# Cross-attention of a decoder layer: all eight key blocks split into high and low parts, three probability buffers, two copies on VectorE's queue

## The reference

```python
query = _layernorm(x)                       # (4, 512, 512)
Q = (query @ Wq).reshape(b, 512, 4, 4, 32)  # 16 query heads in 4 groups
K = (ctx @ Wk).reshape(b, 1024, 4, 32)      # 4 key heads
V = (ctx @ Wv).reshape(b, 1024, 4, 32)
scores = einsum('bqghd,bkgd->bghqk', Q / sqrt(32), K) + m * rel   # a slope for each head
scores = where(mask, scores, neg)
w = softmax(scores, axis=-1)
out = einsum('bghqk,bkgd->bqghd', w, V).reshape(b, 512, 512) @ Wo
x = x + out
```

## Time and profile before

| | us |
|---|---|
| three runs, median (lowest to highest) | 1869.34 (1868.5 to 1874.75) |
| profiled execution, its own time | 1871.28 |
| its span, first to last instruction | 1869.4 |

### The profile page before, as it was taken

One profiled execution on the slowest core, in us unless ns is written; L12 is line 12 of the kernel. 1 busy time (PEld: TensorE's weight loads), 2 busy tenths in 40 slices (PEclk: granted clock), 3 DMA queues, 4 the chain that ended last, 5 costly groups with the idle time before them and its releaser, 6 DMA issues. The chain is left out here.

```text
span 1869.4 us, 24714 instructions
## 1 busy us (share of the span) xinstructions
PE 1663.9 (89%) x8118; PEld 1161.0 (62%) x8118; DVE 1163.6 (62%) x1997; ACT 1213.6 (65%) x1979; POOL 1177.1 (63%) x1080
## 2 busy tenths in 40 slices
PE   6999999999999958999999999999999606999996
PEld 3588888888888735556555655566656302666664
DVE  2366666666766536666855576556757266677764
ACT  2366666656665524887876687667869344788775
POOL 0478777877877503675755576556757306888892
PEclk9999999999999978999999999999999958999999
DMA  6100000000000055112210311120100080010000
GB/s 215 46 12 12 13 20 16 12 12 24 12 7 12 6 171 138 31 26 76 57 43 26 88 31 40 32 49 18 43 23 23 29 315 0 12 35 27 31 18 24
DMA packets 47103, 85.40 MB, mean 46 GB/s; under 512 B 7548, under 2 KB 12028, under 8 KB 45952
## 3 DMA queue, kind: packets, MB, share of 16 engines
q1 hardware_dynamic: 45136, 82.67, 14.3%
q10 hardware_dynamic: 1840, 1.14, 0.2%
HBM read 52.26 MB, written 12.58 MB: 35 GB/s over the span
## 5 line engine op out<-in xcount | busy, mean ns | idle before, releaser
L1146 POOL TENSOR_TENSOR x_p_lo<-x_p,x_p_hi 128x1024 fp32r<-128x1024 f32 x192 | 455.4, 2384 | 300.2 <-ACT x_p_hi L980 299.5
L1095 DVE TENSOR_REDUCE x_maxes<-x_ps_a 128x1 f32<-128x1024 f32 x256 | 313.1, 1223 | 258.1 <-PE x_ps_a L1229 257.2
L958 ACT ACTIVATE x_p<-x_ps_b,x_any_valid 128x1024 f32<-128x1024 f32 x256 | 284.9, 1113 | 168.5 <-PE x_ps_b L1217 167.8
L1217 PE MATMUL x_ps_b<-x_Q,x_K 100*128 100x512 f32 x512 | 228.1, 526 | 3.7 <-ACT x_p L958 2.2
L980 ACT ACTIVATE x_p_hi<-x_p 128x1024 fp32r<-128x1024 f32 x192 | 203.1, 1058 | 4.8
L1229 PE MATMUL x_ps_a<-x_K,x_Q 99*128 99x512 f32 x512 | 166.3, 406 | 6.8 <-DMA x_Q<-x_p_lo 3.9
L1255 PE MATMUL x_ps_o<-x_p_hi,x_V 128*96 128x512 f32 x384 | 157.1, 409 | 1.2 <-POOL x_p_lo L1146 1.2
L1256 PE MATMUL x_ps_o<-x_p_lo,x_V 128*96 128x512 f32 x384 | 150.9, 393 | 0.0
L1217 PEld LDWEIGHTS x_ps_b<-x_Q,x_K 100*128 100x128 f32 x512 | 90.1, 191 | 97.3 <-issue 76.1
L331 ACT ACTIVATE a_work<-a_ps_s,a_neg_max,a_q_r 128x256 f32<-128x256 f32 (+1 forms) x256 | 134.0, 538 | 4.7 <-DVE a_neg_max L419 4.7
L1260 PE MATMUL x_ps_o<-x_p,x_V 128*96 128x512 f32 x256 | 120.4, 591 | 0.0
(11 more groups left out here) (256 smaller groups left out, 4300.9 us busy)
## 6 DMA issues: line engine op xcount, KB each, us to landing
a_w_raw<-in_L_attn_out_w SPq DMA_DIRECT2D x8, 1024.0 KB, 7.8
x_ctxT<-in_ctx SPq DMA_DIRECT2D x8, 1024.0 KB, 7.3
x_Q<-x_q_hi SPq DMA_DIRECT2D x104, 64.0 KB, 2.0
a_xt<-in_x SPq DMA_DIRECT2D x16, 256.0 KB, 2.8
x_scratch<-a_work SPq DMA_DIRECT2D x16, 256.0 KB, 2.0
x_xt<-x_scratch SPq DMA_DIRECT2D x16, 256.0 KB, 3.6
x_K<-x_k_hi SPq DMA_DIRECT2D x32, 128.0 KB, 2.3
x_x1t<-x_scratch SPq DMA_DIRECT2D x16, 256.0 KB, 3.0
```

Of the source, the lines that this page charges most:

```text
L958: act.activation(p[:, r, :, :], ps_b[:, :, :], ACT.Exp, scale=any_valid[:, b % 2:b % 2 + 1]).then_inc(exp_ready, 1)
L1095: dve.tensor_reduce(out=maxes[:, h2, r, 3:4], in_=ps_a[:, :, :], axis=mybir.AxisListType.XY, op=ALU.max)\
L1146: pool.tensor_tensor(out=p_lo[:, r], in0=p[:, r], in1=p_hi[:, r].bitcast(F32), op=ALU.subtract).then_inc(lo_ready, 1)
L1217: last = pe.matmul(ps_b[:, j, :], K[0:ROWS + 4, g, kb * P:(kb + 1) * P], Q[0:ROWS + 4, hh, :], start=True, stop=True)
```

## The change

Four things, all in `phase_cross_attention`:

1. The last two key blocks are treated as the other six: `V` holds eight blocks, `V32` is gone, and at r = 3 ScalarE rounds, GpSimd subtracts and TensorE makes four fp32r matmuls in place of the fp32 ones.
2. `p` has three buffers in place of four, taken in turn over all units, and `p_hi` and `p_lo` have four in place of three. The exponential of a unit waits for the subtraction three units back.
3. The two 32x512 copies that end a head are made by VectorE with `tensor_copy` (function `copies`) at r = 3, before the reciprocal, in place of ScalarE.
4. The mask row lies in rows of `pv_lo` that nothing else uses. It keeps its waits and its two DMAs for each group.

```diff
-        V = sb("V", [P, 2, 6, GX, 3 * DH], F32R)
-        V32 = sb("V32", [P, 2, 2, GX, 3 * DH])
+        V = sb("V", [P, 2, KB, GX, 3 * DH], F32R)
-        p = sb("p", [P, 4, 2, T])
-        p_hi = sb("p_hi", [P, 3, 2, T], F32R)
-        p_lo = sb("p_lo", [P, 3, 2, T], F32R)
+        p = sb("p", [P, 3, 2, T])
+        p_hi = sb("p_hi", [P, 4, 2, T], F32R)
+        p_lo = sb("p_lo", [P, 4, 2, T], F32R)
...
@@ scalar
-                    if c and r < 3:
-                        act.wait_ge(lo_ready, 3 * (c - 1) + r + 1)
-                    if c and r == 3:
-                        act.wait_ge(pv_done, 4 * c)
-                    act.activation(p[:, r, :, :], ps_b[:, :, :], ACT.Exp, ...
+                    if v >= 3:
+                        act.wait_ge(lo_ready, v - 2)
+                    act.activation(p[:, v % 3, :, :], ps_b[:, :, :], ACT.Exp, ...
...
-                if r == 3 and c >= 1:
...
-                    act.activation(pv_lo[0:DH, :], ps_o[k % 2][DH:2 * DH, :], ACT.Copy)...
...
-                    act.activation(den[j * DH:(j + 1) * DH, G % 2, :], ps_o[k % 2][2 * DH:3 * DH, :], ACT.Copy)...
-                if work and r < 3:
+                if work:
...
-                    act.activation(p_hi[:, r], p[:, r], ACT.Copy).then_inc(hi_ready, 1)
+                    act.activation(p_hi[:, r], p[:, v % 3], ACT.Copy).then_inc(hi_ready, 1)
@@ vector
+            def copies(k):
+                j, G = k % HPG, k // HPG
+                dve.wait_ge(pv_done, 4 * k + 4)
+                if k >= 1:
+                    dve.wait_ge(num_ready, k)
+                dve.tensor_copy(pv_lo[0:DH, :], ps_o[k % 2][DH:2 * DH, :]).then_inc(o_copied, 1)
+                if j == 0 and G >= 2:
+                    dve.wait_ge(aT_ready, G - 1)
+                dve.tensor_copy(den[j * DH:(j + 1) * DH, G % 2, :], ps_o[k % 2][2 * DH:3 * DH, :]).then_inc(o_copied, 1)
...
+                if r == 3 and c >= 1:
+                    copies(c - 1)
                 if r == 3 and c >= 5:
                     inverse((c - 5) // HPG, (c - 5) % HPG)
@@ gpsimd
-                if 0 <= c < HEADS and r < 3:
-                    pool.wait_ge(hi_ready, 3 * c + r + 1)
+                if 0 <= c < HEADS:
+                    pool.wait_ge(hi_ready, v + 1)
                     if c:
                         pool.wait_ge(pv_done, v - 3)
-                    pool.tensor_tensor(out=p_lo[:, r], in0=p[:, r], in1=p_hi[:, r].bitcast(F32), op=ALU.subtract)...
+                    pool.tensor_tensor(out=p_lo[:, r], in0=p[:, v % 3], in1=p_hi[:, r].bitcast(F32), op=ALU.subtract)...
@@ tensor
-                    if rw < 3:
-                        pe.wait_ge(lo_ready, 3 * kw + rw + 1)
-                        for j in range(2):
-                            vs = V[:, bw % 2, 2 * rw + j, gw, :]
-                            pe.matmul(bank[0:ROWS, :], vs, p_hi[:, rw, j], start=(rw == 0 and j == 0), stop=False)
-                            last = pe.matmul(bank[0:ROWS, :], vs, p_lo[:, rw, j], start=False, stop=False)
-                    else:
-                        pe.wait_ge(exp_ready, w + 1)
-                        for j in range(2):
-                            last = pe.matmul(bank[0:ROWS, :], V32[:, bw % 2, j, gw, :], p[:, 3, j], start=False, stop=(j == 1))
+                    pe.wait_ge(lo_ready, w + 1)
+                    for j in range(2):
+                        vs = V[:, bw % 2, 2 * rw + j, gw, :]
+                        pe.matmul(bank[0:ROWS, :], vs, p_hi[:, rw, j], start=(rw == 0 and j == 0), stop=False)
+                        last = pe.matmul(bank[0:ROWS, :], vs, p_lo[:, rw, j], start=False, stop=(rw == 3 and j == 1))
```

More of the change, by code:

```diff
@@ L671, in phase_cross_attention @@
         mask_u8 = sb("mask_u8", [P, S], U8)
-        mask_row = sb("mask_row", [P, 512])
         any_valid = sb("any_valid", [P, 2])
@@ L805, in spread_keys @@
                 for j in range(2):
-                    sp.dma_start(K[ROWS + 2:ROWS + 3, g, j * 512:(j + 1) * 512].bitcast(F32), mask_row[32 * j:32 * j + 1, :])\
+                    sp.dma_start(K[ROWS + 2:ROWS + 3, g, j * 512:(j + 1) * 512].bitcast(F32), pv_lo[2 * DH + 32 * j:2 * DH + 32 * j + 1, :])\
                         .then_inc(k_spread[g], 16)
@@ L920, in evacuate @@
                         act.wait_ge(pv_done, 4 * HX * (b - 1))
[L921 to L927, removed]
+                    act.activation(V[:, b % 2, 4 * i:4 * i + 4, :, 0:DH], ps_j[:, :].rearrange("p (t g d) -> p t g d", g=GX, d=DH),
+                                   ACT.Copy).then_inc(job_hi_ready, 1)
             act.wait_ge(const_in, 48)
@@ L953, in _ @@
                         act.wait_ge(valid_ready, b + 1)
[L954 to L958 removed]
+                    if v >= 3:
+                        act.wait_ge(lo_ready, v - 2)
+                    act.activation(p[:, v % 3, :, :], ps_b[:, :, :], ACT.Exp, scale=any_valid[:, b % 2:b % 2 + 1]).then_inc(exp_ready, 1)
                 done = finished_at.get(unit_before(c, r))
@@ L977, in _ @@
                         act.wait_ge(pv_done, v - 3)
-                    else:
+                    elif r < 3:
                         act.wait_ge(q_spread[r], 192)
-                    act.activation(p_hi[:, r], p[:, r], ACT.Copy).then_inc(hi_ready, 1)
+                    act.activation(p_hi[:, r], p[:, v % 3], ACT.Copy).then_inc(hi_ready, 1)
         @block.vector
@@ L1011, in mask_to_row @@
                 for j in range(2):
-                    dve.tensor_scalar(mask_row[32 * j:32 * j + 1, :], mask_u8[32 * j:32 * j + 1, j * 512:(j + 1) * 512],
+                    dve.tensor_scalar(pv_lo[2 * DH + 32 * j:2 * DH + 32 * j + 1, :], mask_u8[2 * DH + 32 * j:2 * DH + 32 * j + 1, j * 512:(j + 1) * 512],
                                        MASKED, MASKED, ALU.mult, ALU.subtract).then_inc(mask_ready, 1)
@@ L1032, in evacuate @@
                     dve.wait_ge(job_hi_ready, highs_until[(name, i, b)])
-                    tiles = 4 if i == 0 else 2
-                    at = V[:, b % 2, 4 * i:4 * i + tiles, :, :]
-                    dve.tensor_tensor(out=at[:, :, :, DH:2 * DH],
-                                      in0=ps_j[:, 0:tiles * P].rearrange("p (t g d) -> p t g d", g=GX, d=DH),
+                    at = V[:, b % 2, 4 * i:4 * i + 4, :, :]
+                    dve.tensor_tensor(out=at[:, :, :, DH:2 * DH], in0=ps_j[:, :].rearrange("p (t g d) -> p t g d", g=GX, d=DH),
                                       in1=at[:, :, :, 0:DH].bitcast(F32), op=ALU.subtract).then_inc(job_read, 1)
@@ L1061, in _ @@
                 if done[0] in ("K", "Q", "V"):
-                    highs += 2 if done[:2] == ("V", 1) else 1
+                    highs += 1
                     highs_until[done] = highs
@@ L1141, in _ @@
                 v, b, hh = 4 * c + r, c // HX, c % HX
-                if 0 <= c < HEADS and r < 3:
-                    pool.wait_ge(hi_ready, 3 * c + r + 1)
+                if 0 <= c < HEADS:
+                    pool.wait_ge(hi_ready, v + 1)
                     if c:
                         pool.wait_ge(pv_done, v - 3)
-                    pool.tensor_tensor(out=p_lo[:, r], in0=p[:, r], in1=p_hi[:, r].bitcast(F32), op=ALU.subtract).then_inc(lo_ready, 1)
+                    pool.tensor_tensor(out=p_lo[:, r], in0=p[:, v % 3], in1=p_hi[:, r].bitcast(F32), op=ALU.subtract).then_inc(lo_ready, 1)
                 if r == 3 and c >= 8 and c % HPG == 0:
@@ L1201, in _ @@
             pe.wait_ge(q_rows_ready, 1)
-            pe.wait_ge(ones_ready, 4)
+            pe.wait_ge(ones_ready, 2)
             before = 0
```

3 lines of the change are left out of this document (removed).

## The result

| | us |
|---|---|
| before, median of 4 runs | 1869.70 (1868.50 to 1874.75) |
| after, median of 4 runs | 1909.15 (1905.38 to 1915.29) |
| ratio, 95% interval | 1.0209 (1.0175 to 1.0242) |
| profiled execution after: own time, span | 1915.29, 1913.2 |

The forecast was 1878 with a range up to 1893. The sign is right, the size is not. The interval lies wholly above 1, but 2% lies within it. The spans differ by 43.8 us, the forecast sum was 8.6.

What follows compares the result with a forecast made beforehand. TensorE bounds streaming units of job heads, VectorE their r = 0; VectorE's and GpSimd's loops lie close to heads without a job. Terms sum to +8.6 us on 1871.3, 1879.9, or 1878 against the median; range 1859 to 1893.

Steps and rivals of the forecast that it cites:

- TensorE's 0.78 a head: Last key pair: cheaper fp32r weight loads save 0.78 us a head, on the path only at r = 2 of job heads.
- The wait for `aT`: Heads 21, 37, 53: output job waits for `normalise` behind the fourth subtraction; +0.8 each for 21 and 37, together +3.4 us.
- the 23 job heads: Heads with a job after a job evacuated by VectorE: -0.78 plus 0.55 or 0.48 us each, -6.1 together.
- The step that failed first: VectorE's copies at r = 3: 0.61 us each, 1.22 together, with neighbours overlapping by 0.08; next maximum 0.55 late.
- VectorE cascades: Rival: copies 0.1 us longer each, or a wait between them, in some 55 heads: +11 to +16, 1890 to 1894; 13%.
- the signs set for being wrong: Copies under 0.45 or over 0.75 us start to start, changed subtraction duration, or clock leaving 1.00 between 760 and 1400.
- I expect 1.00, the 2.4 GHz level: Granted clock in the new heads without a job stays 1.00, with TensorE busy 8.0 of 9.6 us, 83%.
- The clock falls: Rival: in heads without a job 8 us of matmuls become 16, +154 us, 2030; 2%.
- Mask row, memsets: Same waits and DMAs, memsets shrink by a few tenths while VectorE waits for a load anyway: no effect.
- the rival of copies and subtraction that exclude each other: GpSimd's head grows by 1.2 to 11.0 us; 24 heads without a job +1.2 each: 1907; 4%.
- no blocking is seen, and I count none: GpSimd's subtraction takes 2346 to 2431 ns in all 192 cases whatever VectorE does beside it; no port blocking counted.
- From head 57 to the last output projection: Last stretch: GpSimd's 28 subtractions and one `normalise` add 4.0 us, with the reciprocal before the numerator +5.0.

Runs made afterwards that it cites:

- experiment 3: Changed kernel with VectorE's two copies moved from r = 3 to r = 0 of the next head, behind the evacuation: 1877.23 us, ratio 1.0028 to the kernel before.
- Experiment 11: Changed kernel with both copies reading and writing rows 0 to 31, same instructions and sizes, some results unused: 1883.58 us, ratio 1.0068 to the kernel before.
- experiment 4: Changed kernel with two unused filler matmuls before the first piece of a job that follows a job: 1901.87 us, ratio 1.0167 to the kernel before.
- experiment 10: Changed kernel with copies at r = 0, mask rows on ScalarE, normalise first, statistics and valid test moved, plus filler matmuls in heads 3, 19, 35, 51, 53: 1856.00 us.
- experiment 6: Kernel before with only the mask rows moved from r = 3 to r = 1 of head 2 of a sequence, beside a subtraction: one run, 1872.87 us.
- experiment 5: Changed kernel with the mask rows made by ScalarE, behind its rounding at r = 3, not VectorE: 1908.67 us, ratio 1.0181 to the kernel before.
- experiment 2: Kernel before with only the two copies moved to VectorE's queue at r = 3: 1953.65 us, ratio 1.0442.

## Why the prediction was wrong in size, point by point

**Right.** TensorE's 0.78 a head is there (12.58 in experiment 3 against 13.37), and r = 2 of a plain job head takes 2.72 us for a forecast 2.73. The place of the limit is right: VectorE before the maximum of r = 0. The four subtractions and the ring of three cost plain job heads nothing (12.58 again, with both in place). The wait for `aT` in heads 21 and 37 is +1.05 against +0.8. The copies themselves do not wait for GpSimd: 681 to 693 ns in all cases. The sign of the whole, slower, is right, but its largest group, the 23 job heads, has the wrong one.

**The step that failed first: "starts of neighbours follow 0.08 us before the end of the one before (...), so I take 0.61 each, 1.22 together".** The overlap was read from pairs that start in the same rows and carried over to copies that do not. The chain came out at 3.68 for 3.27, 0.41 too little in every head where VectorE ends last, some 45 of 63 by my walk: an estimate of 18 us. With the falls of the clock it turned the 23 job heads from a gain of 6.1 into a loss. The nearest row was a poor neighbour in this one property. For the copies a value that nearly fits, 0.70, stood in the text as the bound "if nothing overlaps"; the range was built with the middle. That covers half of the 0.41; the other half is the maximum's 1.26 for 1.14 and the reciprocal's 0.99 for 0.91, which had no bound. The rival "VectorE cascades" had copies 0.1 us longer and was given 13%; its 1890 to 1894 is still 15 us short. Of the signs set for being wrong this one stayed silent, as the copies start 0.71 us apart and the limit was 0.75; the time of unit r = 0, forecast at 4.5 us and 4.93 in head 23, would have shown it. The trace of before had the sign. Its row of maxima, which is written to rows 96 to 99, starts 1.26 us after a maximum; the reciprocal in the earlier trace rows starts 1.14 after one. Timeline of VectorE, kernel before, head 18:

```profile
929.22 1.23 DVE L1095 TENSOR_REDUCE x_maxes<-x_ps_a 128x1 f32<-128x1024 f32 x1 [0.53 <-PE x_ps_a L1229]
930.48 0.68 DVE L1104 CAST x_Q<-x_ps_x 4x512 fp32r<-4x512 f32 x1
```

The Trainium skill (VectorE: DVE Perf Modes, "Two Vector instructions with no wait between them") has the rule: an instruction whose input or output starts in another group of 32 partitions than the last one in that memory is held until all earlier ones have ended. Experiment 11 agrees, 0.60 against 0.71, and so do the reciprocals of the kernel after, 0.61 behind a copy to row 0 and 0.72 behind the others.

**The second: "I expect 1.00, the 2.4 GHz level".** I argued from TensorE's busy share and looked at heads without a job. There it stayed 1.00 in the kernel after. It fell in job heads, whose waits at r = 0 grew to 1.81 us and more. Seven falls make some 12 us: six of them are the 10.6 us of experiment 4 (5.8 of it in heads 3, 19 and 35), the seventh, head 53, is an estimate from experiment 10's 1.6 in that head. The rival "The clock falls" had the wrong place and price. Falls may also be behind the wider spread of after, 1905 to 1915: its four runs rank by their mean granted clock (0.962, 0.960, 0.959 and 0.956 for 1905.4, 1907.9, 1910.4 and 1915.3 us). Which falls differ was not looked at, as only one of them has a trace.

**The third: "*Mask row, memsets.* Same waits ... nothing".** Same waits, but a new neighbour: GpSimd now subtracts at r = 3. Heads 3, 19 and 35 cost 9.9 us in place of 1.0, of which experiment 4 gives 5.8 to the clock. The conversions wait for the subtraction that runs (experiment 6 and the 2.82 us of experiment 3). I had looked only at GpSimd's durations, the side that went first, and asked the question only of the copies: the rival of copies and subtraction that exclude each other came true for other instructions. So "no blocking is seen, and I count none" was read on the wrong side. The waiting side was in the trace of before, in the variances of the statistics (L998), 128x4:

```profile
L998 DVE TENSOR_SCALAR x_ln_var<-x_mv x4: 158/1014/1867, 671.3 to 1124.3; 128x4 f32<-128x4 f32 x4
```

The Trainium skill (SBUF — State Buffer, "Who interferes with whom") names `tensor_scalar` among the operations that can take the shared ports, and says that whichever instruction comes first keeps them and the other blocks fully. The traces agree, for both of these `tensor_scalar` lines (up to 1.87 and 2.38 us beside a subtraction). One case stays open: in experiment 6 a GpSimd instruction of 128x4, recorded as 1.03 us from 744.11, held neither conversion of the pair at 744.25.

**Smaller.** From head 57 to the last output projection it is +7.7 against +5.0. Of that 4.2 us lie behind the last exponential, in the last product, copies and reciprocals, at half clock in part.

**The sum of the misses.** By the table the 35.2 us between 43.8 and 8.6 lie in the 23 job heads (12.1), the heads after the mask row (8.9), the 14 heads without a job (3.8), the end (2.7), the stretches before head 1 and after the last projection's start (3.4, unexplained), and the rest (about 4.4). By cause my estimates are 18 for the held copies, 12 for the clock, about 3 for the mask row and 2.7 for the end. That these come to 35.7 is partly luck: they leave out the 3.4, and the held copies of heads 57 to 61 are counted in the end too. The causes also act on each other: in experiments 4, 5 and 11 removing one moved falls of the clock to other heads.

**Open.** What decides which of two heads with the same wait loses the clock. Why two falls followed waits of 1.37 us. Why heads without a job in experiment 2 grew by 1.4 us, where the chain explains 0.8.

## What to carry to other kernels

Price an instruction on a full VectorE by its start to start from a row that begins in the same partitions as its neighbours, or else as if nothing overlapped. When an operation moves in time, look at who runs beside it on GpSimd, and look at the longest duration of the operations that may wait, not of the one that holds. A wait of TensorE that has grown can cost more than itself: here 1.4 to 1.6 us each time the clock fell for one stretch, in seven of 31 waits of 1.8 us or more in the kernel after. Moving the two copies by one unit made most of the waits short again; short filler matmuls kept the clock through those that stayed (experiment 10), though in experiment 4 two falls moved to heads without filler.
